# Cross-attention and mixture-of-experts kernel: small statistics operations moved to GpSimd, one normalisation shared by two engines, first weights and one router product moved in their queues

## What is computed

```
x = x + xattn(layernorm(x), fside, ctx)            # per batch: x_q @ w_q.T twice, scales, silu(gate) * up
h = layernorm(x)                                   # [2048, 512]
logits = h @ gate_w.T                              # [2048, 8]
sel = top_k(logits.sum(axis=0), 2)                 # two experts for all tokens
rw  = softmax(logits[:, sel], axis=1)
y   = gelu(h @ w1[sel] + b1[sel]) @ w2[sel] + b2[sel]
x = x + sum_k rw[:, k] * y[k]
```

## Time and profile before

| | |
|---|---|
| runs of the kernel | 825.21 us median of 3 (824.71 to 827.88) |
| the profiled execution | 823.26 us, span 821.4 us |
| busy share of the span | PE 94%, PE weight load 76%, DVE 59%, POOL 54%, ACT 43% |
| chain that ended last | PE 82%, DVE 9%, POOL 4%, issue 3% |
| granted TensorE clock, mean | 0.976 of full speed |

### The profile page before, as it was taken

One profiled execution on the slowest core, in us unless ns is written; L12 is line 12 of the kernel. 1 busy time (PEld: TensorE's weight loads), 2 busy tenths in 40 slices (PEclk: granted clock), 3 DMA queues, 4 the chain that ended last, 5 costly groups with the idle time before them and its releaser, 6 DMA issues.

```text
span 821.4 us, 11341 instructions
## 1 busy us (share of the span) xinstructions
PE 775.2 (94%) x3570; PEld 624.4 (76%) x3577; DVE 487.6 (59%) x693; ACT 355.2 (43%) x660; POOL 445.9 (54%) x473
## 2 busy tenths in 40 slices
PE   5778866999999999999999999999999999999998
PEld 4656543688788888888888888888888888888886
DVE  6999979797754545454545454545454545454545
ACT  3958687733442424242424242424242424242422
POOL 1678898158564646464646464646464646464622
PEclk9799986999999999999999999999999999999999
DMA  9400000301000000000101010101010101000022
GB/s 345 171 1 1 1 1 1 128 1 36 17 27 25 28 24 28 23 28 23 28 23 29 22 30 21 31 20 29 22 32 19 30 21 31 20 31 20 0 103 102
DMA packets 19077, 32.33 MB, mean 39 GB/s; under 512 B 872, under 2 KB 11240, under 8 KB 18160
## 3 DMA queue, kind: packets, MB, share of 16 engines
q1 hardware_dynamic: 18896, 31.98, 11.3%
q10 hardware_dynamic: 160, 0.08, 0.0%
HBM read 27.87 MB, written 4.19 MB: 39 GB/s over the span
## 4 chain that ended last, share of the span: by engine, by line
PE 82%; DVE 9%; POOL 4%; issue 3%; DMA 1%; ACT 1%; ACTq 0%; DVEq 0%; POOLq 0%
PE slot L781 42%; PE slot L768 34%; PE slot L826 3%; DVE rmax L1192 2%; DVE xf L1249 1%; DVE peak_x L1192 1%; POOL res L373 1%; DVE peak_a L1192 1%; DVE xf L1260 1%; DMA b_rows<-in_L_ffn_b 1%; POOL cv L348 1%; DVE stats L1183 1%; POOL rstd L333 1%; POOL h_lo L450 1%; PE slot L563 1%
## 5 line engine op out<-in xcount | busy, mean ns | idle before, releaser
L768 PE MATMUL slot<-xo,a_hi 128*128 128x512 f32 x840 | 259.0, 389 | 0.0
L1513 DVE SCALAR_TENSOR_TENSOR res<-slot,rw,res 128x512 f32<-128x512 f32 x256 | 178.5, 751 | 130.3 <-PE slot L781 130.2
L1542 DVE TENSOR_TENSOR e<-slot,e 128x512 f32<-128x512 f32 x150 | 103.8, 692 | 173.4 <-PE slot L768 173.3
L781 PE MATMUL slot<-w_hi,h_hi 128*128 128x512 f32 x512 | 201.0, 393 | 0.4 <-POOL h_lo L450 0.4
L781 PE MATMUL slot<-w_lo,h_hi 128*128 128x512 f32 x512 | 199.4, 389 | 0.0
L781 PE MATMUL slot<-w_hi,h_lo 128*128 128x512 f32 x512 | 199.3, 389 | 0.0
L768 PEld LDWEIGHTS slot<-xo,a_hi 128*128 128x128 f32 x840 | 157.3, 188 | 33.4 <-DVE e L1542 0.2
L450 POOL TENSOR_TENSOR h_lo<-e,h_hi 128x512 fp32r<-128x512 f32 x96 | 138.2, 1453 | 55.3 <-ACT e L1070 54.3
L768 PE MATMUL slot<-xo,a_lo 128*128 128x512 f32 x420 | 163.4, 389 | 0.0
L781 PEld LDWEIGHTS slot<-w_hi,h_hi 128*128 128x128 f32 x512 | 96.1, 188 | 25.2 <-POOL h_lo L450 5.6
L781 PEld LDWEIGHTS slot<-w_hi,h_lo 128*128 128x128 f32 x512 | 96.1, 188 | 20.2
(11 more groups left out here) (145 smaller groups left out, 825.3 us busy)
## 6 DMA issues: line engine op xcount, KB each, us to landing
raw<-in_L_ffn_w SPq DMA_DIRECT2D x32, 512.0 KB, 3.4
res<-in_x SPq DMA_DIRECT2D x4, 1024.0 KB, 11.8
wv<-in_fside_BxS2xS SPq DMA_DIRECT2D x4, 1024.0 KB, 12.7
out_x<-res SPq DMA_DIRECT2D x3, 1024.0 KB, 3.9
cv<-in_ctx SPq DMA_DIRECT2D x4, 512.0 KB, 13.0
out_x<-res SPq DMA_DIRECT2D x4, 256.0 KB, 2.7
b_row<-in_L_ffn_b SPq DMA_DIRECT2D x2, 256.0 KB, 4.6
b_rows<-in_L_ffn_b ACTq DMA_DIRECT2D x1, 64.0 KB, 5.8
```

What stands on the lines that cost most here:

```text
L768: last = t.matmul(dst, a[:, i, k, :], xo[tp][:, v, k, :], start=(start and n == 0), stop=(n == 3 * H - 1), skip_group_check=True)
L781: last = t.matmul(y_bank[j][:, :], a[:, i, j * P:(j + 1) * P], v[:, f, :], start=(start and n == 0), stop=(not start and n == 2), skip_gro ...
L1513: v.scalar_tensor_tensor(out=r, in0=y_bank[j][:, :], scalar=rw[:, ds(p, 1), n:n + 1].rearrange("p a b -> p (a b)"), in1=r, op0=ALU.mult, o ...
L1542: v.tensor_tensor(dst[:, :], src, other[:, :], ALU.add).then_inc(comb_ready, 1)
```

## The change

It has four parts, and nothing else is touched.

1. For the five statistics steps that DVE makes (`BN_STATS`), the negated mean and the variance plus epsilon are computed by POOL in `inv_std`. DVE's `moments` ends with `bn_aggr`. POOL waits for itself ahead of the power and behind it.
2. Of batch 2, second round, POOL normalises the first two tiles of 128x512 and ACT the other two, in a new call `normalise_rest(2)`.
3. On ACT, `normalise(3, 2)` stands ahead of `keep_full(2, 0)`, and `first_weights` ahead of `keep_hi` of batch 3; `keep_summed(3, 1)` stands ahead of `keep_hi(2, 1)`, and the logits of batch 2 are kept later. On DVE, `first_weights` and `pick_bias` stand ahead of `keep_lo` of batch 3.
4. On PE, `router(3)` stands behind the first tile, `plain(0, 0)`.

```
+        BN_STATS = ((0, 1), (1, 1), (1, 2), (2, 2), (3, 2))
...
             def inv_std(b, c):
                 pool.wait_ge(var_ready[b], c)
-                g.tensor_tensor(rstd[c - 1][b][:, :], var_e[c - 1][b][:, :], neg_half[:, :], ALU.pow
-                                ).then_inc(rstd_ready[b], 1)
-                pool.wait_ge(rstd_ready[b], c)
+                if (b, c) in BN_STATS:
+                    g.tensor_scalar(nmean[c - 1][b][:, :], mv[b][:, :, 0], -1.0, None, ALU.mult)
+                    link(g.tensor_scalar(var_e[c - 1][b][:, :], mv[b][:, :, 1], LN_EPS, None, ALU.add))
+                link(g.tensor_tensor(rstd[c - 1][b][:, :], var_e[c - 1][b][:, :], neg_half[:, :], ALU.pow))
                 g.tensor_tensor(nmr[c - 1][b][:, :], nmean[c - 1][b][:, :], rstd[c - 1][b][:, :], ALU.mult
                                 ).then_inc(nmr_ready[b], 1)
...
             def normalise(b):
                 pool.wait_ge(nmr_ready[b], 2)
-                for j in range(TT):
+                for j in range(H):
...
+            def normalise_rest(b):
+                act.wait_ge(nmr_ready[b], 2)
+                for j in range(H, TT):
+                    s.activation(xv[b][:, j, :], res[:, b * TT + j, :], ACT.Identity, bias=nmr[1][b][:, j:j + 1],
+                                 scale=rstd[1][b][:, j:j + 1]).then_inc(xn_rest, 1)
...
             router(2)
-            router(3)
...
                     plain(tp, 0)
+                    if tp == 0:
+                        router(3)
                     plain(tp, 1)
...
             keep_full(1, 1)
+            normalise_rest(2)
             keep_hi(1, 0)
+            normalise(3, 2)
             keep_full(2, 0)
-            normalise(3, 2)
             keep_hi(1, 1)
             keep_summed(2, 1)
             keep_full(3, 0)
             keep_hi(2, 0)
             keep_logits(0)
+            keep_summed(3, 1)
             keep_hi(2, 1)
-            keep_summed(3, 1)
+            s.activation(gelu_warm[:, :], half[:, 0:1], ACT.Gelu_apprx_tanh)
+            first_weights()
             keep_hi(3, 0)
             keep_hi(3, 1)
-            s.activation(gelu_warm[:, :], half[:, 0:1], ACT.Gelu_apprx_tanh)
-            keep_logits(2)
-            first_weights()
             keep_logits(1)
-            keep_logits(3)
             act.wait_ge(raw2_load, 16)
             down_hi(1)
             down_hi(0)
+            keep_logits(2)
+            keep_logits(3)
...
                 for j in range(TT):
                     ins = v.bn_aggr(mv[b][:, j, :], stats[b][:, j, :])
-                link(ins)
-                v.tensor_scalar(nmean[c - 1][b][:, :], mv[b][:, :, 0], -1.0, None, ALU.mult)
-                v.tensor_scalar(var_e[c - 1][b][:, :], mv[b][:, :, 1], LN_EPS, None, ALU.add).then_inc(var_ready[b], 1)
+                ins.then_inc(var_ready[b], 1)
...
             keep_lo(2, 1)
+            first_weights()
+            pick_bias()
             keep_lo(3, 0)
             keep_lo(3, 1)
-            first_weights()
-            pick_bias()
             first_down_weights()
             pick_logits()
```

More of the change, by code:

```diff
@@ L217, in xattn_ffn @@
         gwt_ps, gwt_ready = sem("gwt_ps"), sem("gwt_ready")
-        var_ready, rstd_ready, nmr_ready = each("var_ready"), each("rstd_ready"), each("nmr_ready")
+        var_ready, nmr_ready = each("var_ready"), each("nmr_ready")
         xn_ready, xn2_ready = each("xn_ready"), each("xn2_ready")
@@ L226, in xattn_ffn @@
         hi_ready, lo_ready = each("hi_ready"), each("lo_ready")
-        res_last, xn_last = sem("res_last"), sem("xn_last")
+        res_last, xn_last, xn_rest = sem("res_last"), sem("xn_last"), sem("xn_rest")
         part_ready, tok_ready, t4_sum = each("part_ready"), sem("tok_ready"), sem("t4_sum")
@@ L329, in _, with link @@
                             pattern=[[-1, P]], channel_multiplier=1).then_inc(consts_ready, 1)
+            links = [1]
+            def link(ins):
+                links[0] += 1
+                ins.then_inc(pool_link, 1)
+                pool.wait_ge(pool_link, links[0])
             def inv_std(b, c):
                 pool.wait_ge(var_ready[b], c)
-                g.tensor_tensor(rstd[c - 1][b][:, :], var_e[c - 1][b][:, :], neg_half[:, :], ALU.pow
-                                ).then_inc(rstd_ready[b], 1)
-                pool.wait_ge(rstd_ready[b], c)
+                if (b, c) in BN_STATS:
+                    g.tensor_scalar(nmean[c - 1][b][:, :], mv[b][:, :, 0], -1.0, None, ALU.mult)
+                    link(g.tensor_scalar(var_e[c - 1][b][:, :], mv[b][:, :, 1], LN_EPS, None, ALU.add))
+                link(g.tensor_tensor(rstd[c - 1][b][:, :], var_e[c - 1][b][:, :], neg_half[:, :], ALU.pow))
                 g.tensor_tensor(nmr[c - 1][b][:, :], nmean[c - 1][b][:, :], rstd[c - 1][b][:, :], ALU.mult
@@ L625, in normed2 @@
                         pe.wait_ge(xn_last, j - H + 1)
+                    elif b == 2 and j >= H:
+                        pe.wait_ge(xn_rest, j - H + 1)
                     else:
```

## The result

| | before | after |
|---|---|---|
| median | 824.88 us (822.13 to 827.88, 22 runs) | 828.16 us (825.68 to 831.99, 22 runs) |
| profiled execution | 823.26 us, span 821.4 | 826.80 us, span 824.9 |
| mean granted clock | 0.976 | 0.975 |

The ratio is 1.0035, 95% interval [1.0024, 1.0045]: the change makes the kernel 2.9 us slower (2.0 to 3.7). The medians lie 3.3 us apart, inside this interval, and the two profiled executions 3.5. Of the long run behind 200 us nothing is lost, so all of it must lie ahead of that. I follow it through the same places as the prediction.

The account below looks back on a forecast made before the run. PE, busy 616.92 of 621 us from 200 us on, was taken as the bound, so earlier losses count one for one. Start 0.25, drain 1.5 and router(3) 3.0 sum to +4.75 on 825.21: 830.0 us, range 826.8 to 833.0.

Parts of the forecast that it names:

- the first rival: POOL and DVE meetings cost nothing and keep_lo comes in time: +2.1 to +3.4 us, 827.3 to 828.6; chance 0.24.
- the signs named beforehand: Expected in the changed profile, such as keep_full of slot 2 ending at 144 or later and second tile 4 to 5.5 later.
- The start, +0.25: Batch 0's statistics: POOL's two small operations and one more hand-over put its power at about 11.87, not 11.62.
- GpSimd's path to batch 3's factors: POOL's queue from residual additions to batch 3's scale factors: ready at 141.5, against 141.84 before.
- The port rule: VectorE and GpSimd's shared ports lock per instruction: factors at 142.2, sum 0.7 higher; the prediction did not follow it.
- The drain of slot 2, +1.5: On ACT, keep_full(2, 0) now behind batch 3's normalisation: PE's 16 transposes start at 144.3, not 142.82.
- The first weights, 0 to 0.1: Weights ahead of batch 3 on ACT and DVE: first tile gains 0 to 0.1 us relative to the choice; taken as 0.
- `router(3)`, +3.0: Behind the first tile on PE: its 2.14 us no longer hidden, plus waits for keep_lo; range 2.1 to 3.2.
- The clock stays up: PE at 2.4 GHz instead of half clock from 131 to 146.7: -1.05 us, 824.2; chance 0.08.
- The clock falls behind the pause: PE's pause ahead of the first tile drops first tiles to half clock: 2 to 3 us more, 832 to 833; chance 0.10.
- Meetings cost nothing: The first rival: POOL and DVE do not delay each other, keep_lo in time; +2.1 to +3.4 us, chance 0.24.

Follow-up runs that it names:

- e9: Same kernel as e6 (only batch 2's normalisation shared, against the kernel before), run in turn with e10 on one chip: 822.91 us, ratio 0.9971.
- e3: Changed kernel with router(3) back ahead of the first tile and part 3 undone except normalise(3, 2) ahead of keep_full(2, 0): 825.65 us, ratio 1.0012.
- e4: As e3, but keep_full(2, 0) again ahead of normalise(3, 2) on ScalarE: 824.85 us, ratio 0.9992.
- e2: Changed kernel with router(3) put back ahead of the first tile, first weights still ahead of keep_lo of batch 3: 833.28 us, ratio 1.0115.
- e5: Kernel before with part 1 only: small statistics operations on GpSimd, which still normalises all four tiles of batch 2: 827.46 us, ratio 1.0020.
- e7: Changed kernel with part 3 undone except the place of normalise(3, 2); router(3) still behind the first tile: 829.62 us, ratio 1.0052.
- e1: Kernel before with only router(3) moved behind the first tile: 827.61 us, ratio 1.0031.
- e10: Same kernel as e8, run in turn with e9 on one chip: 822.98 us, ratio 0.9974.
- e6: Kernel before with part 2 only: GpSimd and ScalarE share batch 2's normalisation, keep_full(2, 0) ahead of normalise(3, 2): 824.17 us, ratio 0.9983.
- e8: As e6, with the small statistics operations of batch 1, second round, alone on GpSimd: 822.28 us, ratio 0.9975.

## Why the prediction was right, and where it was off

The direction was right and the 828.16 lies inside the range, 1.8 us under the forecast of 830.0. The order of causes held as well: `router(3)` first, the drain second. The sizes did less well. The band of the forecast itself, +3.4 to +5.9 (828.6 to 831.1), just misses the median; that falls into the band of the first rival. The chances had put 0.49 on a loss of over 0.5% and 0.45 on less, and it was 0.35%. Of the signs named beforehand one did not come: the second tile was to start 4 to 5.5 us later and started 3.5 later. Step by step:

- *The start, +0.25: a term that did not arrive.* GpSimd's power for batch 0 starts at 12.11, not 11.62: 0.49 late, twice my figure, though 0.13 of it was there before the statistics began (8.52, not 8.39). GpSimd's two operations and their hand-overs take 0.62 (11.49 to 12.11), where VectorE's took 0.32 (11.30 to 11.62), and they begin 0.19 later (that 0.13 and 0.06); I had counted the operations and one hand-over. But all of it is gone at 73.04 (73.06 before), where VectorE's clip took 0.17 instead of 0.69, and GpSimd's six additions start at 121.71 against 121.74. In the two profiled executions the term is 0. The other runs scatter too much there to say it for the median.
- *GpSimd's path to batch 3's factors.* Forecast 141.5, measured 141.43. The pieces were off by up to 0.8, in both directions, so the nearness of their sum is luck. I had VectorE's additions go first and GpSimd's second wait; in fact both engines were slowed (3.08 and 2.94), and GpSimd was through at 133.95, not 134.75. The gain was spent on its negated mean of 134.04, which took 0.56, and on its second normalisation, which took 1.8.
- *The port rule.* By "SBUF — State Buffer", section "SBUF: two separate sides", of the Trainium skill, the power would have kept VectorE's `keep_lo` out for its whole duration. The trace does not agree: the power of 139.67 lasted 1.04 and `keep_lo` started inside it at 140.15 and lasted 1.23, as it does alone. What waited was GpSimd's product of 140.78, which came second (0.65 instead of 0.20), until `keep_lo` was done. The runs show the other order too: in e9 `keep_lo` started at 139.88 and the power at 140.05, and the power took 1.91.
- *The drain of slot 2, +1.5.* 1.37 at the transposes; e3 against e4 confirms the cause. At the choice only 1.03 is left. The mean granted clock from 146 to 150 was 0.85 before and is 0.75 after. Between the levels 0.50 and 1.00 that puts the rise at 147.2 and at 148.0 (an estimate from these means): 0.8 us later, while the work came 1.4 later, so more of it ran at 2.4 GHz. The stretch from the transposes to `sum_row` took 6.49 us, not 6.83.
- *The first weights, 0 to 0.1: a term that hangs on the transfer.* The reading itself holds: before, the weights landed at 154.97, 3.7 us after their issue, and ScalarE took them at 155.07, with its queue full up to that point. In the changed kernel they landed after 3.4 us and ScalarE stood ready. So the distance from issue to `a_hi` went from 3.80 to 3.39, and that is how 1.03 at the choice became 0.62 at the tile. Most of these 0.4 us is the transfer: over the twelve traces it takes 3.4 to 3.7 us. In e2, with ScalarE in the order of the changed kernel, it was a slow one, ScalarE waited 2.22 for it, and `a_hi` came 3.75 after the issue (152.52). But a fast transfer helps only where the queue lets it through: in e5 and e7, with the old order and a landing of 3.4, `a_hi` came 3.81 after the issue. So this move is worth 0.1 to 0.4 us in these traces, by the transfer; 0 was read off one execution with a slow one. That `router(3)` cost nothing in its old place is confirmed by e1.
- *`router(3)`, +3.0.* From the first tile's start to the second's it was 2.82 us and is 5.74: +2.92. Wait, matmuls and order were as forecast.
- *Rivals.* "The clock stays up" did not come: 0.50 from 131 to 142. In e10 it came in part (1.00 from 140 to 146), the 16 transposes took 2.4 us instead of 3.9, and little of it reached the tile, for ScalarE's drains were in the way. "The clock falls behind the pause" did not come in the changed kernel, whose pause is 1.86 us, nor in e1 (2.58), but it came in e7 (2.58) and e2 (5.96). "Meetings cost nothing" gave 827.3 to 828.6 and holds the median, but not for its reason: the meetings did cost, and it was the start, the clock's rise, the weights and small change at the drain and the router that gave 1.2 us back. Nothing cancelled there: all five misses lie on one side. And the transfer of 3.4 us is that of one execution.

The lines of three of these readings: before, the clock from 146 to 150, and ScalarE's queue ahead of `a_hi`; in e2, `a_hi`.

```profile
146.00:150.00 4.00, 4.00 (x23) 2.40 (x22) 3.12 (x6) 2.47 (x5) 0.00 (x0) 0.85 0.00 0
```

```profile
153.20 1.28 ACT L1058 ACT_TABLE_LOAD   x1
...
154.61 0.56 ACT L953 COPY logits<-slot 16x512 f32<-16x512 f32 x1
```

```profile
156.27 1.32 ACT L973 CAST a_hi<-raw 128x256 fp32r<-128x256 f32 x4 [2.22 <-DMA raw<-in_L_ffn_w]
```

In the profiled execution 3.5 us stand against the forecast sum of 4.75: 0.25 from the start, 0.13 from the drain, 0.34 from the clock, 0.41 from the weights and 0.08 from the router. Of the median's 1.8, 0.3 is its base (824.88 over 22 runs, not 825.21 over 3), and the medians lie 3.3 apart, which leaves 1.5 for these terms.

What stays open: whether the start term is there in the median; why the clock fell in e7 and not in e1; and how e7's difference from the changed kernel divides. Its one trace gives 0.6 at the first tile (0.4 of it ScalarE's queue) and 1.3 for the clock, less the 0.8 of the wait, 1.1 in all.

## What to carry to other kernels

A wait whose cause the profile names can have a second gate at the same height. Before, the first tile had three at nearly the same height: the landing of the weights, ScalarE's queue and `router(3)`. Read such a distance in several executions before pricing a move: here the transfer alone varied by 0.3 us, and ScalarE's queue decided whether that counted.

Freeing an engine that is not the bound by giving its small operations to the one that is costs time (e5), and moving a drain behind a wait costs that wait to whoever needs the buffer (e3 against e4). Work that lies in a pause of PE is free there and dear one place later (e1). Two moves in different queues can depend on each other: the weights' move alone was 6.6 us slower than with `router(3)` moved too (e2), and yet the best kernels here have neither (e6, e9, and e8, e10).

One trace of each kernel is not enough to price 1 us: e1 came 1.3 late in code that it did not change.

## What the runs showed of the hardware

- Two engines in back-to-back operations on two SBUF tensors both pay: VectorE's two additions took 3.08 us instead of 1.29 beside GpSimd's two at 2.94 instead of 2.50.
- A small VectorE operation (128x4, 0.17 elsewhere) that comes while GpSimd adds tensors back to back waits until one of its additions ends, and not always the next: 1.31 us before, 3.75 in e1, for the same operation of the same code.
- A power on 128x4 was not disturbed by a VectorE operation that started behind it (1.04), and nearly doubled by one that started ahead of it (1.91 in e9).
- The granted clock on PE around a pause: still 1.00 behind 1.86 us (changed kernel) and behind 2.58 us (e1); down from about 1.4 us into the tile behind another pause of 2.58 us (e7, an estimate from the mean of 0.54 from 160 to 162); down in the pause itself in one of 5.96 us (e2).
- The load of the first weights, 512 KB, landed 3.4 to 3.7 us after its issue: 3.4 in the changed kernel and 3.7 in e2, whose orders on SyncE and ScalarE are the same.
- Executions of one and the same program differ by over 1 us in where the first part ends: e8 and e10, the same kernel, have their six residual additions at 121.27 and 122.49.
